# Attention scores on TensorE: sixteen matmuls of 64 x 32 per head group in place of eight of 64 x 64

## What is computed

```python
DIM, H, KV, HD, WIN = (256, 16, 4, 64, 128)
x = x + attn(layernorm(x)); x = x + ffn(layernorm(x))
# in attn
q = rmsnorm((x @ wq.T).reshape(B, T, H, HD), q_norm_w)
k = rmsnorm((x @ wk.T).reshape(B, T, KV, HD), k_norm_w)
scores = jnp.einsum('bqhd,bkhd->bhqk', q, k) / jnp.sqrt(64)   # k, v repeated 4 times over the heads
mask = (i >= j) & (i - j < WIN)
attn = softmax(where(mask, scores, -inf))
y = einsum('bhqk,bkhd->bqhd', attn, v).reshape(B, T, H * HD) @ wo.T
```

## Time and profile before

| | |
|---|---|
| median of three runs (lowest, highest) | 2423.83 us (2421.53, 2424.13) |
| the profiled execution's own time | 2420.27 us |
| its span, first to last instruction | 2418.6 us |
| PE busy | 2380.1 us, 98% |
| DVE, ACT, POOL busy | 89%, 89%, 54% |
| chain that ended last | 97% PE |

### The profile page before, as it was taken

The page is one execution under the profiler, slowest core; times in us unless marked ns, Lnnn a source line. Parts: engine busy times, 40 slices in busy tenths (PEclk is TensorE's granted clock), DMA queues, the critical chain, the costliest instruction groups (busy, mean ns, idle before and its releaser), DMA issues.

```text
span 2418.6 us, 70409 instructions
## 1 busy us (share of the span) xinstructions
PE 2380.1 (98%) x25856; PEld 1958.6 (81%) x25856; DVE 2152.0 (89%) x5736; ACT 2160.9 (89%) x7687; POOL 1309.6 (54%) x1771
## 2 busy tenths in 40 slices
PE   6999999999999999999999999999999999999997
PEld 4888888888888888888888888888888888888886
DVE  6899899999988999999999899989999998999886
ACT  5899989999998999899989989998999899899996
POOL 3555555555555555555555555555555555555542
PEclk9999999999999999999999999999999999999999
DMA  2000000000000000000000000000000000000000
GB/s 70 13 15 19 15 15 16 18 15 15 19 15 15 15 19 15 15 15 19 15 15 19 16 15 15 19 15 15 15 20 15 15 17 18 15 15 19 13 9 12
DMA packets 39729, 41.23 MB, mean 17 GB/s; under 512 B 4448, under 2 KB 38624, under 8 KB 39392
## 3 DMA queue, kind: packets, MB, share of 16 engines
q1 hardware_dynamic: 39392, 36.73, 5.0%
HBM read 19.93 MB, written 16.78 MB: 15 GB/s over the span
## 4 chain that ended last, share of the span: by engine, by line
PE 97%; issue 1%; ACT 1%; POOL 1%; DVE 1%; DMA 0%; SPq 0%; POOLq 0%
PE ps_a L633 17%; PE ps_scores L676 14%; PE ps_y L695 12%; PE ps_d L629 7%; PE ps_d L627 7%; PE ps_d L628 7%; PE ps_y L710 5%; PE ps_b L629 5%; PE ps_b L627 5%; PE ps_b L628 5%; PE ps_d L633 3%; PE ps_c L629 2%; PE ps_c L628 2%; PE ps_c L627 2%; PE ps_c L633 1%
## 5 line engine op out<-in xcount | busy, mean ns | idle before, releaser
L330 ACT ACTIVATE probs<-merged,neg_max 128x128 f32<-128x128 f32 x2048 | 796.0, 394 | 0.5 <-DVE neg_max L491 0.5
L253 POOL TENSOR_SCALAR_AFFINE_SELECT pT_other<-pT 128x256 f32<-128x256 f32 x384 | 173.1, 451 | 606.4 <-ACT pT L345 606.4
L237 POOL TENSOR_TENSOR q_r<-q_ve,minus_half 128x8 f32<-128x8 f32 x256 | 420.3, 1642 | 92.4 <-DVE q_ve L467 92.4
L676 PE MATMUL ps_scores<-kT,qT 64*64 64x192 f32 (+2 forms) x8192 | 415.2, 311 | 1.0 <-DVE merged L481 0.6
L330 ACT ACTIVATION_READ_ACCUMULATOR probs<-merged,neg_max 128x1 f32 x2048 | 396.5, 194 | 0.0
L481 DVE COPY_PREDICATED merged<-later_key,ps_scores 128x512 f32<-128x512 int32 x384 | 284.7, 741 | 106.2 <-ACT merged L323 106.2
L345 ACT ACTIVATE pT<-ps_a 128x512 f32<-128x512 f32 x512 | 306.2, 598 | 62.0 <-PE ps_a L633 61.1
L491 DVE TENSOR_REDUCE neg_max<-merged 128x4 f32<-128x512 f32 x512 | 346.5, 677 | 4.5
L695 PE MATMUL ps_y<-pT,values 128*64 128x128 f32 x4096 | 337.0, 285 | 1.8 <-ACT pT L345 1.8
L633 PE MATMUL ps_a<-ident,probs 128*128 128x128 f32 x2048 | 336.4, 287 | 0.0
L676 PEld LDWEIGHTS ps_scores<-kT,qT 64*64 64x64 f32 x8192 | 262.7, 133 | 60.6 <-issue 32.8
(11 more groups left out here) (114 smaller groups left out, 6175.7 us busy)
## 6 DMA issues: line engine op xcount, KB each, us to landing
xs<-x SPq DMA_DIRECT2D x128, 128.0 KB, 2.2
out<-ob SPq DMA_DIRECT2D x128, 128.0 KB, 1.7
w_plain<-w_qkv SPq DMA_DIRECT2D x3, 512.0 KB, 5.0
w_plain<-w_o SPq DMA_DIRECT2D x8, 128.0 KB, 5.3
w_plain<-w_ffn SPq DMA_DIRECT2D x1, 392.0 KB, 5.7
w_plain<-w_v SPq DMA_DIRECT2D x1, 128.0 KB, 4.9
nw<-norm_w SPq DMA_DIRECT2D x1, 1.0 KB, 5.5
```

The lines of the kernel that those rows point to most:

```text
L237: pool.tensor_tensor(q_r[:, T % DEEP, c], q_ve[:, T % DEEP, c], minus_half[:, 0:8], ALU.pow).then_inc(s_qr[n], 1)
L330: last = nc.scalar.activation(probs[:, r, h], merged[:, r, h], ACT.Exp, bias=neg_max[:, r, h:h + 1], accum_out=den[:, r, h:h + 1])
L676: last = nc.tensor.matmul(ps_scores[queries, 2 * half + c, first:end], qT[rows, T % 2, 2 * g + c, queries], kT[rows, g // 2, at + first:at ...
```

## The change

The queries of a group are cut in four blocks of 32 instead of two of 64. Each block takes the keys that its window can reach, 160 in place of 192, or at slot 0, 32, 64, 96 and 128. A call then uses a tile of 64 x 32 of the array, one eighth of it, and a group has 16 calls instead of eight. Nothing else differs: the lists of DVE, ACT, POOL and SP are the same row for row.

```diff
                 for c in range(2):
-                    for n in range(2):
-                        queries = slice(HD * n, HD * n + HD)
-                        first, end = (HD * n if slot(T) else P), P + HD + HD * n
+                    for n in range(4):
+                        queries = slice(32 * n, 32 * n + 32)
+                        first, end = (32 * n if slot(T) else P), P + 32 + 32 * n
                         at = (T % WIDE - 1) * P
                         for half in range(2):
                             rows = slice(HD * half, HD * half + HD)
```

## The result

The changed kernel takes 2448.61 us (median of four runs, 2447.36 to 2451.33) beside 2423.38 for the kernel before in the same session: a ratio of 1.0107 (95% interval 1.0089 to 1.0124), 25 us slower. The forecast was 2444 us, range 2416 to 2514.

A forecast was written before the change was run, and what follows sets the result against it. The prediction took TensorE (PE, 97% of the chain) as the bound. Shorter rounds -41, new borders +61, the fixed part and other engines 0 gave +20 us on the 2423.83 us median: 2444 us, range 2416 to 2514.

The forecast's parts named there:

- Term 1: Scores, 384 groups with 192 keys: four rounds each 27 ns shorter at 160 keys, 41 us less; slot 0 gains nothing.
- Term 2: Between scores and attend_other (L710), 380 places: array tile kinds now differ, a fixed 0.16 us is paid twice, 61 us more.
- Term 3: Fixed part of 512 score groups at 64 x 32: half the weight load, longer stagger of eight tiles; nothing, bounds -13 to +13 us.
- Term 4: DVE, ACT and POOL do the same work, hidden behind PE: cost zero; otherwise a buffer wait would show at L676.
- No border: Between 64 x 32 scores and 64 x 64 attend_other nothing is paid, so term 2 is zero: 2383 us; chance 0.10.
- a cheaper border: Between scores and attend_other only 0.09 us is paid per border, 34 us in all: time 2417 us; chance 0.07.
- streams that don't run at once: In the scores, four key streams don't go at once, so four more rounds a group: +262 us, 2706; chance 0.06.
- the issue bound: Score matmuls can't be issued faster than 27 ns each, a group takes 0.86 us: +178 us, 2622; chance 0.05.
- the late round: In the scores, the last tiles of a group start one round late: +69 us on top of the sum, 2513; chance 0.06.

The follow-up runs named there:

- the run with the borders alone: Kernel before with only attend_other cut to 64 x 32 array tiles, scores left at 64 x 64 with 192 keys: 2482.62 us, ratio 1.0246.

## Why the prediction was right, and where it was short

**Term 1, shorter rounds, -41 us.** Right. A lone group fell by 0.11 us, and with 192 keys on the same tiles it went back to 0.81.

**Term 2, new borders, +61 us.** Right, and shown by itself: +61 us with nothing else changed, 52 us back when the border was taken out of the changed kernel although waits of 4 us more came with it.

**Term 3, the fixed part of 64 x 32, zero.** Right in both halves: the load fell from 50 to 26 ns, the start of eight tiles takes some 50 ns and not 20, and 0.70 us is four rounds of 0.135 and 0.16.

**Term 4, other engines, zero.** This step was short by 5 us. It said that shorter groups, "0.1 us", stand among other PE work and are covered. The cover was taken from busy shares and never read at each reader: low_x came just in time already, as its reader's load started 0.12 us after it, with the wait and without. The four groups of a tile at slot 1 are 0.43 us shorter with no border in that tile, and in the tile after it low_x did not come that much sooner, in part because L502 grew by 0.18 us beside centre_x. Each load was 0.18 us late, 30 times. The step looked for trouble at the buffer of L676, and it came at a weight load of L627. 20 + 5 = 25 us, which is what was measured. The run with 64 x 32 at slot 1 alone shows which tile brings the wait, and the run with h_statistics later shows that the wait was the missing part. How the 0.18 us part between PE's lead and the longer L502 no run shows.

**The rivals.** No border and a cheaper border are excluded by the run with the borders alone, streams that don't run at once and the issue bound by the 0.81 us of 32 matmuls with 192 keys, and the late round by the 0.70 us of a lone group.

## What to carry to other kernels

Before an operation is cut to fit its data better, look at what stands beside it on TensorE: its array tile is shared with its neighbours, and a saving of 0.11 us a group was lost to a border of 0.16. Cut the neighbour the same way and the saving comes out. And when a stretch of the bound engine gets shorter, add up the lead over the whole tile and set it against the slack of each producer that it reads. Slack is counted from the time at which a waiting reader could start, here 0.12 us after the producer's end, and not from that end. Look at the producer place by place too, as a mean over all places hid a wait that had only moved. A call of the producer that nobody waits for soon can go behind the one that is late, but ask the same of each call that is passed.

## What the runs showed that was not expected

32 float32 matmuls and as many weight loads ran in 0.54 us of rounds, 17 ns a matmul, with eight tiles at once; before the change the densest stretch had 27. DVE instructions of one form differ by where they stand: L502 took 0.69 us at most places and 0.95 at one, and L456's mean went from 612 to 470 ns when a GpSimd instruction moved. And with attend_other ahead of scores at slot 0, both 64 x 32, the pair took 0.87 us where the other order fits 0.82; why was not tried.
